# Attention on one core: the four value products of a step issued as two halves, behind the second and the fourth score product of the next step

## What is computed

```python
q, k, v = split(x @ Wq.T + bq), split(x @ Wk.T + bk), split(x @ Wv.T + bv)   # 2 x 16 heads, 2048 x 16 each
cross_kv = jnp.cross(k3, v3, axis=-1)
scores = (einsum('bhqd,bhkd->bhqk', q, k) + einsum('bhqc,bhkc->bhqk', q_stp, cross_kv)) * temp
attn = softmax(scores, axis=-1)
out = einsum('bhqk,bhkd->bhqd', attn, v)
return out.transpose(0, 2, 1, 3).reshape(Bx, Tx, Dx) @ Wo.T + bo
```

## Time and profile before

| | |
|---|---|
| median of the runs | 3949.27 us |
| the profiled execution | 3957.01 us |
| its span | 3955.2 us |
| mean granted TensorE clock | 0.934 of full |
| first and last start of a value product | 2144.5 and 3649.9 us |
| TensorE's matmul time over the span | 3451.3 us (87%) |
| VectorE, ScalarE, POOL | 2949.9, 2202.5, 1519.5 us |

### The profile page before, as it was taken

How to read it: one execution, slowest core, us unless ns; L and a number is a source line. 1 busy time by engine, 2 the same in 40 slices (tenths; PEclk the granted TensorE clock), 3 DMA queues, 4 the chain that set the end, 5 groups by cost and what they waited for, 6 DMA issues and landing times. The chain is left out here.

```text
span 3955.2 us, 50070 instructions
## 1 busy us (share of the span) xinstructions
PE 3451.3 (87%) x14561; PEld 1589.3 (40%) x14561; DVE 2949.9 (75%) x3567; ACT 2202.5 (56%) x3624; POOL 1519.5 (38%) x1292
## 2 busy tenths in 40 slices
PE   3348888898888889898958999999999999999898
PEld 1115545454554545455621233333223323233566
DVE  3898787888878787884128888888878888888343
ACT  4436555555556545554112777777777777777221
POOL 1988778787777878786010000000000000000110
PEclk8669999898999989999976999999999999999999
DMA  2111213121121312212103000000000000001000
GB/s 97 31 38 48 62 55 106 56 86 67 59 67 56 106 54 76 75 58 103 51 32 96 21 18 18 18 18 18 18 18 18 20 23 19 18 18 34 21 28 30
DMA packets 110953, 183.09 MB, mean 46 GB/s; under 512 B 14624, under 2 KB 84792, under 8 KB 102010
## 3 DMA queue, kind: packets, MB, share of 16 engines
q1 hardware_dynamic: 110713, 180.20, 14.3%
HBM read 154.05 MB, written 26.09 MB: 46 GB/s over the span
## 5 line engine op out<-in xcount | busy, mean ns | idle before, releaser
L1700 DVE TENSOR_REDUCE tile_max<-ps 128x1 f32<-128x1024 f32 x1076 | 1267.7, 1220 | 254.7 <-PE ps L1483 251.9
L1641 ACT ACTIVATE probs<-ps 128x512 f32<-128x512 f32 x2056 | 1116.2, 599 | 457.0 <-PE ps L1497 431.3
L1182 POOL TENSOR_TENSOR h<-h,c_sb 128x512 f32<-128x512 f32 x512 | 684.8, 1369 | 329.8 <-DVE state L996 329.7
L990 DVE TENSOR_TENSOR_SCAN h<-decay,state,ps 128x512 f32<-128x512 f32 x512 | 655.1, 1279 | 105.9 <-POOL y_sum L1193 34.1
L1497 PE MATMUL ps<-qs,ks 101*128 101x512 bf16 x2056 | 708.4, 382 | 1.2
L1483 PE MATMUL ps<-ks,qs 99*128 99x512 bf16 x2152 | 664.0, 390 | 49.0 <-DMA ks<-scratch_kb 41.1
L1193 POOL TENSOR_TENSOR y_sum<-y_sum,h 128x512 f32<-128x512 f32 x512 | 638.6, 1279 | 8.7 <-issue 0.2
L1817 POOL COPY vh<-v_all 128x256 f32 (+1 forms) x32 | 12.6, 400 | 1403.4 <-PE ps L1507 1339.8
L1507 PE MATMUL ps<-probs,vh 128*32 128x512 f32 x4096 | 545.6, 605 | 3.5 <-issue 3.5
L539 PE MATMUL ps<-x1T,e_w 128*128 128x512 f32 x1024 | 486.4, 626 | 58.5 <-ACT hid L807 58.5
L561 PE MATMUL ps<-e_w,hid 128*128 128x256 f32 x2048 | 455.4, 381 | 38.4 <-issue 19.0
(11 more groups left out here) (176 smaller groups left out, 2870.7 us busy)
## 6 DMA issues: line engine op xcount, KB each, us to landing
e_w<-in_e_w SPq DMA_DIRECT2D x64, 1024.0 KB, 7.0
c_sb<-scratch_c SPq DMA_DIRECT2D x128, 256.0 KB, 3.3
qs<-scratch_q SPq DMA_DIRECT2D x210, 64.0 KB
ks<-scratch_k SPq DMA_DIRECT2D x210, 64.0 KB
scratch_q<-parts SPq DMA_DIRECT2D x16, 384.0 KB, 4.0
scratch_k<-parts SPq DMA_DIRECT2D x16, 384.0 KB, 4.1
xr<-scratch_x SPq DMA_DIRECT2D x10, 512.0 KB, 4.2
xn_tok<-in_x SPq DMA_DIRECT2D x8, 512.0 KB, 4.9
```

Of the source, the lines that this page charges most:

```text
L990: v.tensor_tensor_scan(h[:, n % 2, m, :], decay[:, n % 2, m, :], ps[:, 0, :], state[:, n, m:m + 1], ALU.mult, ALU.add).then_inc(s["h_ready ...
L1182: last = nc.gpsimd.tensor_tensor(h[:, n % 2, m, :], h[:, n % 2, m, :], c_sb[:, n % C_RING, :], ALU.mult)
L1641: fn(probs[:, step % 2, qc, :], ps[:, S_BANK[i], :], ACT.Exp)\
L1700: v.tensor_reduce(tile_max[:, t, half:half + 1], ps[:, slot(side):slot(side) + PAIR, :].rearrange("p a n -> p (a n)"), AX.X, ALU.max).then ...
```

## The change

`values` gets an argument `half` and issues two of the four products: qc 0 and 1, or qc 2 and 3. Its wait for `probs_ready` is for those two chunks. `av_mm` is counted at the second half. `step_of` gets `behind`, the value products to be issued within it: half 0 behind score product 1 and half 1 behind score product 3. For all steps but step 0 of a head the block of four is replaced by this; step 0's two halves stand one right after the other where its block stood. `turn_max` now comes behind the value products of step 8's body. Nothing changes on the other engines.

```diff
-            def values(u, j, step):
-                if step == 0:
+            def values(u, j, step, half):
+                if step == 0 and half == 0:
                     pe.wait_ge(s["v_staged"], u + 1)
                     at_least(pe, s["av_copied"], u)
-                pe.wait_ge(s["probs_ready"], u * PER_HEAD + (step + 1) * STEP + CREDIT)
-                for qc in range(QC):
+                pe.wait_ge(s["probs_ready"], u * PER_HEAD + step * STEP + 2 * half + 2 + CREDIT)
+                for qc in (2 * half, 2 * half + 1):
                     last = mm(ps[qc * VW:(qc + 1) * VW, AV_BANK, :], vh[:, j, step, :],
                               probs[:, step % 2, qc, :], start=step == 0, stop=step == KT - 1)
-                last.then_inc(s["av_mm"], 1)
+                if half == 1:
+                    last.then_inc(s["av_mm"], 1)
...
-            def step_of(u, r, j, step, use, side):
+            def step_of(u, r, j, step, use, side, behind=None):
...
                 scores(u, j, step, 1)
+                if behind is not None:
+                    values(*behind, 0)
                 scores(u, j, step, 2)
                 next_max(u, r, j, step, 1, use + 1, 1 - side)
                 scores(u, j, step, 3)
+                if behind is not None:
+                    values(*behind, 1)
...
-                    values(u, j, 0)
+                    for half in range(2):
+                        values(u, j, 0, half)
                     for step in range(2, KT):
                         at = turn_use(step, 0)
-                        step_of(u, r, j, step, base + at, (M_BASE + at) % 2)
+                        step_of(u, r, j, step, base + at, (M_BASE + at) % 2, (u, j, step - 1))
                         if step == TURN_STEP:
                             turn_max(base + TURN_USE, (M_BASE + TURN_USE) % 2, u + 1)
-                        values(u, j, step - 1)
                     base = M_BASE + (u + 1) * M_PER_HEAD
                     after, turn = (j + 1) % ROT, r + (j + 1) // ROT
-                    step_of(u + 1, turn, after, 0, base, M_BASE % 2)
-                    values(u, j, KT - 1)
+                    step_of(u + 1, turn, after, 0, base, M_BASE % 2, (u, j, KT - 1))
                     step_of(u + 1, turn, after, 1, base + 2, M_BASE % 2)
                     turn_values(base + FOLD_USE, (M_BASE + FOLD_USE) % 2, u)
```

## The result

The changed kernel takes 4453.41 us (median of four runs, 4446.79 to 4458.72) against 3955.71 for the kernel before on the same occasions: a ratio of 1.1262, 95% interval 1.1236 to 1.1288, 12.6% slower, some 498 us. The profiled execution's span is 4450.5 us, 495.3 more than before.

A forecast was written before the change was run, and what follows sets the result against it. PE's chain of issue was taken to bound the attention; 499 - 7 - 10 = +482 us on the profiled 3957.0 gave 4439, stated as 4432 us for the median of runs, with 4345 to 4525 holding 8 times in 10.

The forecast's parts named there:

- The split: 480 blocks become two halves, each still two passes, 1.065 us against the block's 1.09: 1.04 us more per step, +499 us.
- Switches: Changes between full-width score products and narrow value products: 0.09 us ahead and roughly 0.10 behind, paid by each half.
- The two ends of the split: Low: the extra half pays only its passes, +408 us; high: switches around a half cost twice a block's, +590 us.
- Waits: The halves' waits for their chunks of probs hold nothing up and cost nothing in the stream.
- Last step of a head: Half 0 covers the 0.21 us wait for a chunk ahead of the third score product: 32 x 0.21 = -7 us.
- Step 8: Half 1 covers the 0.30 us wait for VectorE at the row maxima's transpose: 32 x 0.30 = -10 us.
- Step 1: No value products lie inside it, so its wait for VectorE and four transposes stay, 3.72 us.
- the +14: Step 0's block: one more pass, 32 x 0.44 us, if the second half started only at the first's second pass; taken as 0.
- Shares: Rival: two products need half the time of four, so only switches are added: +74, 4023 us; 5%.
- Real waits for ScalarE: Rival: the 610 us of gaps credited to probs are real and early halves fill them: -204, 3745 us; 2%.
- Three passes: Rival: a half's records run strictly in code order, three turns in place of two: +422 more, 4853 us; 4%.
- Clock: Rival: the granted clock falls to 1.2 GHz for half of the attention, time near 5400 us; 3%.

The follow-up runs named there:

- short exponentials: Kernel before, with ScalarE making only the first 256 of each chunk's 512 exponentials, order and waits unchanged: 3958.96 us.
- the pair alone: Kernel before, with two of the four value products left out in steps 1 to 15 of each head: 3954.46 us.
- The tiny product: Kernel before, block whole, plus one tiny fp32 product of zeros behind score product 1 in each of 480 steps: 4083.75 us.
- split alone: Changed kernel with both halves issued one right behind the other where the block stood: 3961.59 us.
- the quarters: Changed kernel split further, one value product behind each of score products 0, 1, 2 and 3: 5487.65 us.

## Why the prediction was right

*The bound.* PE's issue bounds the attention; the list of waits was read rightly as credit without a cost in a plain step, and the 0.21 us in a head's last step rightly as a real one. Shown by the short exponentials.

*The split.* The step that carried the forecast, a half pays by passes and not by products, held: 480 x 1.04 = 499 us forecast, 480 x (3.91 - 2.84) = 514 measured. The size was off by 3% in one term: half = 1.09 - 2 x 0.013 = 1.065. The second pass starts 0.45 us behind the first with two products as with four, so only one of the two 0.013 is saved, and a half is 1.07 to 1.08. Pair and block differ by 0.02 us, as the pair alone showed.

*Switches.* I took 0.09 ahead and 0.10 behind from the rows, 0.19 in all. The tiny product gives 0.22 with what lies between the passes. The two ends of the split, 0.85 and 1.23 us more per step, were both far from the measured 1.07.

*Waits.* Free, as forecast (split alone: no difference).

*Last step of a head.* 3.05 became 3.91, the same as its neighbours: the 0.21 went, -7 us, as forecast.

*Step 8.* Forecast 4.08, measured 4.02. The wait went; the transpose adds 0.11 and not 0.21, so that it is -13 us in place of -10. The starts fit a transpose that counts as full width: it stands 0.98 behind the half, as a score product does (2731.63 to 2732.61), and 0.11 ahead of the next score product, while ahead of value products it took 0.21. By that, the 0.10 between the two is a switch that it no longer adds. No run tried this by itself.

*Step 1.* Forecast unchanged. From its first score product to the value products behind the transposes it is 2.72 us before (2611.59 to 2614.31) and after:

```profile
2701.51 0.39 PE L1497 MATMUL ps<-qs,ks 101*128 101x512 bf16 x1
...
2703.65 0.66 PE L1517 MATMUL ps<-ident,av 128*128 128x128 f32 x4 [0.23 <-DVE tile_max L1704]
2704.23 0.64 PE L1507 MATMUL ps<-probs,vh 128*32 128x512 f32 x4
```

The two halves that follow run as one block (four first passes together), so the +14 that I had left open did not come.

*Sum.* 514 - 7 - 13 = 494 us; the spans differ by 495.3. The forecast was 482, and 4432 us lay 0.5% under the measured 4453. Of these 21 us, 16 are the difference (482 against 498), most of it the half's 0.03 a step; the rest is that the kernel before had 3949 us in the runs of the forecast and 3956 with one run more.

*Rivals.* Shares: refuted by the pair alone and by the quarters. Real waits for ScalarE: refuted by the short exponentials. Three passes: refuted by the four records of a half, two and two (two turns, not three), and by the split alone, where the first passes of the second half ran ahead of the second passes of the first. Clock: 1.00 over the attention, in the changed kernel too. The Trainium skill ("TensorEngine Tiling (Array Packing)", Key Properties) says that a change of the tiling mode drains TensorE. The traces agree that each change costs, at the middle value of the forecast and a little more: 0.22 us for a switch to narrow products and back.

## What to carry to other kernels

Here matmuls that took different column groups of the array cost the passes of one, so a block of them is one unit: two products cost what four cost, and one too (1.05, 1.06 and 1.04 us). Spreading such a block over a stream of full-width products, for the sake of finer waits, multiplies its price by the number of pieces; 0.22 us of each piece's 1.07 is the detour from full width and back. Before a wait is worked around, the step's starts have to be added up: where they leave no slack, the wait that the profile credits costs nothing.

## What the runs showed that I had not expected

A VectorE reduction of 128 x 1024 from PSUM is recorded with 1.20 to 1.23 us, but when its inputs are ready they start every 1.13 us. The recorded lengths overlap, as matmuls' do. A bound for VectorE that is made of recorded lengths (2.45 a step) was 8% too high, and that hid 90 us of what bf16 values could give.

Order within a step matters through VectorE too: the value block is also the pause in which VectorE catches up. Moved to another place, at no cost in a plain step (2.84 us either way), it cost 27 us at the two places of a head where transposes take a bank pair: behind step 8, felt in step 9, and in step 1.
